# A written-out order for every engine from the second last attention step to the first feed-forward tiles

## The reference

```python
x = _L0(x, theta, phi)            # rotation of pairs of channels
x = _L1(x, t, ...)                # two modulated norms and products, silu
x = _L2(x, safety_score, ...)     # low-rank steering
# _L3: transformer block, 16 heads of 32 channels
h = layernorm(x, gamma1, beta1)
Q, K, V = h @ Wq + bq, h @ Wk + bk, h @ Wv + bv          # 16 heads of 32
scores = einsum('bhqd,bhkd->bhqk', Q, K) / sqrt(32)      # causal
ctx = einsum('bhqk,bhkd->bhqd', softmax(scores), V)
x1 = x + ctx @ Wo + bo
h2 = layernorm(x1, gamma2, beta2)
x2 = x1 + gelu(h2 @ W1 + b1) @ W2 + b2                   # 512 -> 2048 -> 512
return x + g[:, None, None] * (x2 - x)
```

## Time and profile before

| what | before |
| --- | --- |
| median of the runs | 1706.26 us |
| profiled execution, its own time | 1705.07 us |
| its span | 1703.3 us |
| mean granted clock of TensorE | 0.976 |
| TensorE busy | 1633.5 us, 96% of the span |
| VectorE busy | 1162.8 us, 68% |
| ScalarE busy | 989.0 us, 58% |
| GpSimd busy | 403.7 us, 24% |

### The profile page before, as it was taken

The page is one execution under the profiler, slowest core; times in us unless marked ns, Lnnn a source line. Parts: engine busy times, 40 slices in busy tenths (PEclk is TensorE's granted clock), DMA queues, the critical chain, the costliest instruction groups (busy, mean ns, idle before and its releaser), DMA issues.

```text
span 1703.3 us, 27189 instructions
## 1 busy us (share of the span) xinstructions
PE 1633.5 (96%) x9318; PEld 1316.6 (77%) x9318; DVE 1162.8 (68%) x2767; ACT 989.0 (58%) x2329; POOL 403.7 (24%) x606
## 2 busy tenths in 40 slices
PE   6799998899999999999999799999999999999999
PEld 4588766667777777777776478878999999999998
DVE  7799865768787878777766448767565656565643
ACT  5688843777777777787877545534242424242432
POOL 5788620222222222222221102020202020101010
PEclk9899998989999999999999799999999999999999
DMA  7122233434444444444344515666746464646451
GB/s 306 60 82 82 86 124 77 129 71 129 99 127 100 126 100 125 103 122 110 95 97 112 198 51 204 247 223 246 257 158 252 161 248 169 247 173 248 173 198 68
DMA packets 61825, 254.78 MB, mean 150 GB/s; under 512 B 10581, under 2 KB 15957, under 8 KB 45945
## 3 DMA queue, kind: packets, MB, share of 16 engines
q1 hardware_dynamic: 61688, 253.06, 45.5%
HBM read 153.93 MB, written 48.23 MB: 119 GB/s over the span
## 4 chain that ended last, share of the span: by engine, by line
PE 85%; DVE 6%; DMA 3%; ACT 2%; issue 1%; SPq 1%; POOL 1%; DVEq 0%; POOLq 0%; ACTq 0%
PE psum L83 22%; PE psum L84 21%; PE psum L85 21%; PE psum L1928 5%; PE psum L1909 5%; PE psum L1956 5%; DMA k_raw<-in_w_in 1%; PE psum L1852 1%; DVE psum L1191 1%; PE psum L1860 1%; PE psum L3082 1%; DMA k_raw<-d 1%; PE psum L1842 0%; PE psum L1827 0%; DMA out<-k_result 0%
## 5 line engine op out<-in xcount | busy, mean ns | idle before, releaser
L1191 DVE CUSTOM_DVE_ANT_0 psum<-psum,b_mask 128x512 f32<-128x512 f32 (+3 forms) x512 | 242.9, 509 | 92.1 <-PE psum L1909 87.6
L1534 ACT ACTIVATE psum<-psum,b_mx 128x512 f32<-128x512 f32 (+3 forms) x512 | 258.0, 506 | 74.3 <-DVE b_mx L1191 71.9
L2991 ACT ACTIVATE k_act<-k_stack_f,k_smalls 128x512 f32<-128x512 f32 x112 | 81.0, 723 | 338.1 <-DVE k_stack_f L2779 338.1
L1544 ACT ACTIVATE k_exps<-psum 128x512 f32<-128x512 f32 (+1 forms) x384 | 196.4, 528 | 84.7 <-PE psum L1928 83.6
L1058 POOL TENSOR_SCALAR_AFFINE_SELECT k_exps<-k_exps 128x256 f32<-128x256 f32 x256 | 96.1, 412 | 458.8 <-ACT k_exps L1544 458.8
L2632 POOL TENSOR_SCALAR k_result<-k_result,k_pb 128x512 f32<-128x512 f32 x32 | 59.9, 1889 | 454.2 <-DVE k_result L2698 454.2
L2758 DVE TENSOR_TENSOR k_act_lo<-k_act,k_act_hi 128x512 fp32r<-128x512 f32 x112 | 77.3, 690 | 130.1 <-ACT k_act_hi L2994 130.1
L1928 PE MATMUL psum<-k_stack 98*128 98x512 f32 (+3 forms) x512 | 141.7, 340 | 12.6 <-ACT k_exps L1544 7.1
L83 PE MATMUL psum<-k_act_hi,k_w_hi 128*128 128x512 f32 x384 | 150.9, 393 | 0.6 <-DVE k_act_lo L2758 0.6
L84 PE MATMUL psum<-k_act_lo,k_w_hi 128*128 128x512 f32 x384 | 150.6, 392 | 0.0
L85 PE MATMUL psum<-k_act_hi,k_w_lo 128*128 128x512 f32 x384 | 150.3, 391 | 0.0
(11 more groups left out here) (377 smaller groups left out, 4445.3 us busy)
## 6 DMA issues: line engine op xcount, KB each, us to landing
k_stack<-w_factors SPq DMA_DIRECT2D x35, 1792.0 KB, 7.7
k_stack<-k_samples SPq DMA_DIRECT2D x384, 128.0 KB, 2.4
k_weights<-w_factors SPq DMA_DIRECT2D x17, 1792.0 KB, 7.7
x<-k_tokens SPq DMA_DIRECT2D x10, 1024.0 KB, 3.9
k_tokens<-x SPq DMA_DIRECT2D x8, 1024.0 KB, 5.2
d<-k_result SPq DMA_DIRECT2D x32, 256.0 KB, 2.9
k_raw<-x SPq DMA_DIRECT2D x8, 1024.0 KB, 4.9
k_raw<-d SPq DMA_DIRECT2D x8, 1024.0 KB, 7.1
```

Of the source, the lines that this page charges most:

```text
L1191: last = dve.tensor_tensor_reduce(got, got, mask[:, S - width:S], -INV_SQRT_DH, -2.0 * MASKED, ALU.add, ALU.min, mx[n % 2][:, h, t:t + 1])
L1534: act.activation(sc(n, u)[:, at:at + width], sc(n, u)[:, at:at + width], ACT.Exp, bias=mx[n % 2][:, h, t:t + 1], scale=-1.0, accum_out=sum ...
L1544: act.activation(exps[n % 2][:, h, at:at + width], by_key(n, u)[:, 0:width], ACT.Exp, scale=INV_SQRT_DH).then_inc(k_act, 1)
L2991: act.activation(act_f[:], whole_tile, ACT.Gelu, bias=small(smalls, "b1", 2 * pair % M + second)).then_inc(pair_gelu, 1)
```

## The change

Nothing that is computed changes; both programs have the same instructions, in the same number, on every engine. Up to step 29 their order is the same too, and the steady pattern is now a loop over `STEADY`. From step 30 to the last feed-forward tile of sample 0 each engine has a function of its own that calls the steps one by one: `sync_tail`, `gpsimd_tail`, `vector_tail`, `scalar_tail` and `tensor_tail`. The general loop, `beside`, `after`, `step(m)` and FIRST_STEPS are gone. The banks of PSUM that the products use in the tail stand in a table (TAIL_USES) in place of `bank_uses_in_turn`. Lines of the changed kernel have other numbers: by key L1928 is L1692, context L1956 is L1722, the maxima rows L968 are L899, the W loads L2188 and L2199.

```diff
+STEADY = range(G, GROUPS - 2)
-                for u in range(STEPS):
-                    if 0 <= n < GROUPS:
-                        score(n, u)
-                    if u not in AFTER_PIECES and 0 <= n - 1 < GROUPS:
-                        score_by_key(n - 1, u)
...
-                    beside(n, u)
...
-                    after(n, u)
+            for n in STEADY:
+                groups[n % G](n, n // G)
...
+def sync_tail(att, ff):
+
+    att.first_after()
+    att.max_rows(29, 1)
+    att.stack_rows(31, (0, 1))
+    att.max_rows(30, 0)
+    att.attention_out(6, 0)
+    att.attention_out(6, 1)
+    att.stack_rows(31, (2, 3))
+    ff.first_weights(0)
+    ff.second_weights(0)
+    att.max_rows(30, 1)
+    att.max_rows(31, 0)
+    att.attention_out(6, 2)
+    att.attention_out(6, 3)
+    att.max_rows(31, 1)
+    ff.second_weights(1)
+    att.attention_out(7, 0)
+    ff.first_weights(1)
+    for k in range(1, 4):
+        att.attention_out(7, k)
+    ff.second_weights(2)
+    ff.pair_in(2)
+    ff.sample_in(1)
...
+def vector_tail(att, ff):
...
+    att.ctx_low(30)
+    ff.w1_low(1)
+    ff.w2_low(0)
+    att.ctx_low(31)
+    ff.split(0)
+    ff.w1_low(2)
+    att.attention_result(7, 0)
+    ff.w2_low(1)
+    ff.w2_low(2)
+    att.attention_result(7, 1)
+    att.attention_result(7, 2)
+    ff.w2_low(3)
+    att.attention_result(7, 3)
+    ff.split(1)
+    ff.start_result(0)
...
+def scalar_tail(att, ff):
...
+    att.exponentials_by_key(30, 6)
+    att.exponentials_by_key(30, 7)
+    att.scale_back(8, 2)
+    att.split_high(0, 8)
+    att.exponentials_by_key(30, 8)
+    att.exponentials(31, 10)
+    att.exponentials(31, 11)
...
+    att.scale_back(8, 3)
+    att.exponentials_by_key(31, 0)
+    att.exponentials_by_key(31, 1)
+    att.split_high(1, 8)
+    ff.w1_high(0)
...
+def tensor_tail(att, ff):
...
+    for k in range(4, 8):
+        att.score_by_key(31, k)
+    ff.first_product(0)
+    att.score_by_key(31, 8)
+    att.score_by_key(31, 9)
+    att.wo_piece(7, 2)
+    att.score_by_key(31, 10)
+    att.score_by_key(31, 11)
+    ff.first_product(1)
+    att.context(31, 0)
+    att.context(31, 1)
+    att.context(31, 3)
+    att.context(31, 2)
+    ff.first_product(2)
+    for k in range(3, 16):
+        att.wo_piece(7, k)
+    ff.second_product(0, 0, 0, 1, 2, 3)
+    ff.first_product(3)
+    ff.second_product(1, 1, 0, 1, 2, 3)
```

More of the change, by code:

```diff
@@ L272, in gpsimd @@
         gs_columns(2)
-        for k in range(B + 1):
-            first, second = AT.get((1, k)), AT.get((0, k + 2))
+        for k in range(PREFIX):
+            first, second = AT[1, k], AT[0, k + 2]
             if k:
                 gs_columns()
[L277 to L282, removed]
+            deviation(first)
+            gs_columns(3)
+            deviation(second)
+        return steps(gs_columns, deviation)
     def vector(dve, ahead):
@@ L702, in tensor @@
         pe.wait_ge(w_lo_set, 1)
-        for n in range(2 * B):
+        for n in range(2 * PREFIX):
             st, b = SEQ[n]
@@ L1322, in ahead, with first_sum @@
-        def ahead(place, part=None):
+        def first_sum(half):
+            if half == 0:
+                dve.wait_ge(sample_ld, 32)
+            for j in (2 * half, 2 * half + 1):
+                dve.tensor_tensor(first[:, j, :], first[:, j, :], first_d[:, j, :], ALU.add).then_inc(mid_set, 1)
+        def ahead(place):
             if place == "start":
                 gate_constants()
-            if (place, part) == (0, 1):
+            if place == "row high":
                 row_high()
-            if (place, part) == (0, 4):
+            if place == "row low":
@@ L2572, in pair_in @@
                 sp.wait_ge(factor_lo, len(parts) * MADE_AT[pair])
+            else:
+                attention["results"](sp)
             for k in range(2):
@@ L3062, in samples @@
                     period(b, p)
-        return after, samples
+        return steps(w1_high, w2_high, factor_high, tokens, scale, block_high, gelu, samples)
     def tensor(pe):
@@ new lines, in gpsimd_head @@
+def gpsimd_head(mod, att):
+    mod.gs_columns(1)
+    mod.deviation(12)
+    mod.gs_columns(3)
+    mod.deviation(13)
+    mod.gs_columns(1)
+    mod.deviation(14)
+    mod.gs_columns(2)
+    mod.deviation(15)
+    att.mask_and_low()
+    att.prepare_rstd(0)
+    att.stacked_ones()
+    att.cut_later(0, 0)
+    att.prepare_rstd(1)
+    att.cut_later(0, 1)
+    att.split(1, 0)
+    att.split(1, 1)
+    att.split(1, 2)
+    att.split(1, 3)
+    att.cut_later(1, 0)
+    att.cut_later(1, 1)
+    att.cut_later(2, 0)
```

2035 lines of the change are left out of this document (1303 added, 732 removed), and 6 rows, old and new, of the table HEAD_USES.

## The result

The changed kernel takes 1696.7 us (median of five runs, 1693.11 to 1697.3) against 1706.26 before: the ratio is 0.9947, with an interval of 0.9926 to 0.9968. That is 9.6 us less by the medians and 9.0 by the ratio (5.5 to 12.6), where 14.2 were forecast. Its profiled execution has a span of 1695.5 us. Run again beside the experiments, the same kernel took 1693.61 us against 1703.65, a ratio of 0.9938 (0.9921 to 0.9955). One further run of the kernel before took 1851.65 us, 8% more than all others, and is not in the ratio.

The account below looks back on a forecast made before the run. TensorE bounds the kernel; waits (15.0 us) and low clock (9.7) lose 24.7 us in the attention's tail. Of these 10.5 stay (2 + 4 + 0.3 + 1.2 + 3), so 14.2 go from 1705.07: 1691 us, range 1683 to 1700.

Parts of the forecast that it names:

- only a third comes back: Rival: ScalarE, late rows, low clock and late halves leave 19 us lost, gain 6, 1699 us; chance 0.20.
- What bounds the kernel: Attention tail, 915.41 to 1000: TensorE's idle 15.0 us and low clock 9.7, together 24.7 at most to win.
- The 3 us for the clock: Attention tail: one short stretch at the lower clock expected, losing 3 us instead of 9.7 (0 to 6).
- the first rival: TensorE full throughout the tail: 1 to 4 us remain, gain 21 to 24, 1682 us; chance 0.15.
- The loads x2 and d: Step 30's first maxima rows: loads issued some 11 us earlier, near 920, so the 5.1 us gap goes.
- W1 and W2 ahead of the rows: Step 30's second half: 3 MB of weights ahead delay its maxima rows; stall 1 to 5 us, taken as 2.
- ScalarE between the scores: Last scores: TensorE's waits for ScalarE's by-key exponentials expected to leave 4 us, between 2 and 6.
- The end: Context of step 31: a first product covers GpSimd's last cut, so the wait is 0.3 us (0 to 0.5).
- Behind 1000: After the tail, where VectorE's and ScalarE's orders also move: counted 0 us, between −2 and +3.
- The slower rival: `split(1)` and `add_attention(1)` on VectorE wait for SyncE's transfers: a loss of 10 us, 1715 us; chance 0.05.
- The signs: Right if: no rows wait at step 30's start, at most 5 us before unit 6, context 31 about 969, clock above 0.92.
- the signs of being wrong: VectorE-ended gap before second product 1 or 5, wait for a half before first product 0, or clock near 0.5 over 10 us.

Follow-up runs that it names:

- e2: Changed kernel with e1's exchange, and on VectorE W2 tiles 4 and 5 and split(2) ahead of start_result(0): 1692.48 us, ratio 0.9938 to the kernel before.
- e3: Changed kernel with W1's second half and W2's third quarter issued behind the stores and the load of pair 2: 1692.27 us, ratio 0.9929 to the kernel before.
- e4: Changed kernel with the loads of x2 and d back in their old place on SyncE: 1704.76 us, ratio 1.0005 to the kernel before.
- e7: Kernel before with only the loads of x2 and d moved early: 1695.53 us, ratio 0.9952 to the kernel before.
- e6: Changed kernel with first products 0 and 1 behind the context of step 31, as before: 1700.18 us, ratio 0.9982 to the kernel before.
- e1: Changed kernel with the W2 halves ahead of the factors of pair 2 on ScalarE: 1695.82 us, ratio 0.9955 to the kernel before.
- e8: Changed kernel with the moves of e2 and e5 together: 1689.42 us, ratio 0.9913 to the kernel before.
- e10: Changed kernel with the moves of e8 and e3 together: 1689.59 us, ratio 0.9910 to the kernel before.
- e9: Changed kernel with e5's move and the feed-forward start in about the old order on TensorE, ScalarE and VectorE: 1685.09 us, ratio 0.9883 to the kernel before.
- e11: e9 with the turns back of tokens 2 and 3 of sample 1 one tile earlier: 1680.07 us, ratio 0.9881 to the kernel before.
- e5: Changed kernel with the maxima rows of step 30's second half ahead of W1 and W2: 1689.68 us, ratio 0.9922 to the kernel before.

## Why the prediction was right, and what it missed

The direction and the range (1683 to 1700) held; the gain was 9.0 to 9.6 of the 14.2 forecast. That the time fell into the range is in part luck. The tail gave more than forecast, and the start, which was counted at 0, took 8 to 10 us. Together about 18 us are left of 24.7; the rival "only a third comes back" has 19, but by causes that did not come.

**What bounds the kernel.** Right: idle time and a clock of 0.52 to 0.57 in three stretches were there to win at the end of the attention. The 9.7 us for the clock in the 24.7 are my estimate, half of the 19.4 busy us in these stretches, and no run shows them as such: at the granted clocks of 0.53, 0.52 and 0.57 it is 9.1, which with the 15.3 us not busy makes 24.4, what the tail before lost. The gain of the tail alone is larger than forecast. After the change TensorE is idle for 3.2 us in 940 to 960 and 1.3 us in 960 to 980, 4.5 in sum up to 998.16, and a clock of 0.83 over 940 to 960 costs about 3.4 more (0.17 of 20 us; 3.1 by windows of 1 us): 7.9 of 24.7 are left, where I had put 10.5. The 3 us for the clock were the right size here, but they are less steady than the idle time: 4.5 in the repeat, 6.1 in e2 and e3, whose tail has the same order. The 63% that the first rival takes as the busiest engine is ScalarE's; TensorE itself was 82% busy (69.33 of 84.59 us).

**The loads x2 and d.** Right in place and size: they were issued at 918.63 and 919.33, and by-key unit 0 of step 30 waits for nothing. e4 and e7 show that this one move carries as much as the whole change does.

**W1 and W2 ahead of the rows.** Issued at 939.91 and 940.59 (939.9 forecast); the rows were there at 950.91 (951.3 forecast), the stall 1.5 (2 forecast). That the small rows might overtake the loads did not happen: they took 11.0 us from the first load's issue. The pace taken for a full queue, about 400 GB/s, is that of the traces: 410 to 434 in 934 to 937 before, while the loads of x2 and d ran, and 424 to 438 in 944 to 948 after. But I priced the stall at 2 us and the clock as a term apart, 3 us for all waits together. The runs with and without this wait show that the two go together: 4 to 7 us.

**ScalarE between the scores.** 1.9 us instead of 4. The cause is open: the two first products are not it, since e6, with both moved away, has 2.0. **The end.** The context started at 972.87 (969 forecast) with no wait of its own; e6 confirms that the first products are the cover.

**Behind 1000: the term that failed.** "I count 0, between −2 and +3." Measured in the first profile: waits of 5.7 and 1.4 us for `split` and 3.1 us of half clock (6.15 busy us at 0.50, the last stretch shown above), 10.2 in sum. The repeat has 8.1 in sum. The tail's gain of 24.7 − 7.9 = 16.8 less 10.2 is 6.6, against 6.9 in the stretch. I had seen that the orders of VectorE and ScalarE move there too, and had only added up their work, which stayed the same. It was the waits in these orders that counted.

**The slower rival** had the kind and the place, not the instruction. The store of (7, 1) did stand behind W1's 2 MB (7.8 us from issue to VectorE's release at 990.21), but `split(1)` was in time at 990.88. The wait came one tile later, through ScalarE and the load of pair 2. I had given this 0.05 as a cause of a slower kernel; as a cause that takes 8 to 10 us of a gain it deserved a term of its own.

**The signs.** No wait at step 30's first by-key unit, 1.50 us before its unit 6, the context without a wait for GpSimd, and a granted clock of 0.96 over 915 to 1000 came as said. The stretches behind were not only shifted, and of the signs of being wrong a gap that VectorE ends came, before second product 2 instead of 1 or 5.

**Why mending it did not pay.** e1, e2, e3, e8 and e10 each shorten or remove a wait that they aim at, and the start still loses 6.5 to 8.9 us; the kernels with the changed order there lose 7.8 to 10.1. The start of the feed-forward part is a chain: results stored, load of pair 2, its factors, load of pair 3, its factors, tokens of sample 1. In the changed order each link stands ahead of work that TensorE needs at once. Only e9, in which TensorE is tiles ahead before ScalarE comes to the first link, gets the time (4.6 us lost, and 0.4 in e11). It moves steps on three engines at once. Which of these moves is needed was not tried apart, so that the lead is what counts is argued, not shown by itself.

## What to carry to other kernels

When a written order moves a step that waits for a load, look at what stands behind it on the same engine and when that is needed, not at the engine's sum of work. Put steps whose data come late behind work that keeps the bounding engine ahead by several tiles. And before a whole section is rewritten, try the one move that the longest wait names: here it gave as much as the whole net gain. Then compare kernels by what the bounding engine loses in each part: two that take the same time can lose it in different places.

## What the runs showed of the hardware

- A wait of 1.5 us in a stretch with other short waits had the clock at 0.83 over 20 us (0.74 in the repeat); without it (e5) the same stretch ran at 1.00, though waits of 1.0, 0.7 and 0.6 us remained.
- How long the clock stayed low behind this wait differed from profile to profile: about 7, 10, 7, 14 and 14 us in the changed kernel, its repeat, e1, e2 and e3, which have the same order there. That cost 3.1 to 6.1 us.
- The part before the change, the same instructions in all of these kernels, ended between 909.4 and 915.0 us in the profiled executions. Two profiled spans are therefore compared from a common instruction on.
- The wait view named ScalarE for an 8.12 us gap (e4) whose cause was a load that VectorE waited for; only the chain through VectorE's row shows it.
